# The causal mask of a score bank: written by ScalarE instead of by an identity product on TensorE

## What is computed

```python
x = x + _layernorm(attn(_layernorm(x)))
x = x + _layernorm(ffn(_layernorm(x)))          # ternary weights, hidden width 2048
# in attn, for each batch and head:
q, k = rope(q), rope(k)
scores = q @ k.T                                 # 512 x 512, where key > query: -inf
attn = softmax(scores) * E ** -0.5
o = attn @ v
```

## Time and profile before

| | |
|---|---|
| Median of 3 runs | 1364.31 us (1363.02 to 1364.67) |
| The profiled execution | 1362.21 us, its span 1360.4 us |
| Granted TensorE clock, mean over the span | 0.951 |
| PE busy | 1205.2 us (89%), 9388 instructions |
| DVE busy | 1025.1 us (75%), 2931 instructions |
| ACT busy | 782.3 us (58%), 1446 instructions |
| POOL busy | 593.8 us (44%), 636 instructions |
| PE on the chain that ended last | 56% of the span |

### The profile page before, as it was taken

One profiled execution on the slowest core, in us unless ns is written; L12 is line 12 of the kernel. 1 busy time (PEld: TensorE's weight loads), 2 busy tenths in 40 slices (PEclk: granted clock), 3 DMA queues, 4 the chain that ended last, 5 costly groups with the idle time before them and its releaser, 6 DMA issues.

```text
span 1360.4 us, 27331 instructions
## 1 busy us (share of the span) xinstructions
PE 1205.2 (89%) x9388; PEld 653.4 (48%) x9388; DVE 1025.1 (75%) x2931; ACT 782.3 (58%) x1446; POOL 593.8 (44%) x636
## 2 busy tenths in 40 slices
PE   4755869999999998999989998999989999988796
PEld 2322545455545554555545554555545554555343
DVE  7588897878887787878877787878877787767532
ACT  3334864666466754666456754666456754666480
POOL 5231432791159312881149412781149412871252
PEclk9865999999999999999989999999989999989799
DMA  5451121002210212002300212002300112001000
GB/s 201 127 153 64 41 62 55 1 4 68 81 38 2 56 53 82 1 18 66 105 3 2 55 46 89 1 14 66 94 18 2 49 48 61 1 2 46 17 2 31
DMA packets 49701, 65.60 MB, mean 48 GB/s; under 512 B 8439, under 2 KB 33047, under 8 KB 49052
## 3 DMA queue, kind: packets, MB, share of 16 engines
q1 hardware_dynamic: 49564, 63.78, 16.1%
HBM read 29.90 MB, written 8.39 MB: 28 GB/s over the span
## 4 chain that ended last, share of the span: by engine, by line
PE 56%; DVE 26%; ACT 7%; issue 6%; POOL 3%; DMA 1%; SPq 1%; POOLq 0%; ACTq 0%; DVEq 0%
PE gen L476 25%; PE down L519 14%; DVE score L1075 5%; PE pv L573 4%; PE score L545 4%; DVE hT L942 2%; PE score L536 2%; DVE acc_add L1052 2%; PE score L551 2%; DVE probs L942 2%; POOL rstd L1407 1%; DVE qkn L1167 1%; DVE mx L1075 1%; ACT qkn L736 1%; PE gen L536 1%
## 5 line engine op out<-in xcount | busy, mean ns | idle before, releaser
L1407 POOL TENSOR_TENSOR rstd<-veps,mhalf 128x1 f32<-128x1 f32 (+1 forms) x104 | 68.4, 657 | 492.9 <-DVE veps L1152 379.9
L792 ACT ACTIVATE probs<-score 128x512 f16<-128x512 f32 (+1 forms) x384 | 201.9, 526 | 127.5 <-PE score L545 127.5
L942 DVE TENSOR_TENSOR probs<-score,probs 128x512 f16<-128x512 f32 (+1 forms) x384 | 213.6, 596 | 65.6 <-ACT score L794 64.6
L476 PE MATMUL gen<-x2T,t1T 128*128 128x512 f16 x1024 | 249.9, 391 | 4.9 <-DVE hT L942 3.4
L519 PE MATMUL down<-t2T,hT 128*128 128x512 f16 x1024 | 232.8, 380 | 3.8 <-DVE xn L1137 3.8
L794 ACT ACTIVATE score<-score 128x512 f32<-128x512 f32 (+1 forms) x384 | 204.7, 533 | 0.0
L476 PE MATMUL gen<-xT,wa 128*128 128x512 f16 x768 | 178.2, 383 | 12.2 <-DVE wa L962 8.4
L942 DVE TENSOR_TENSOR hT<-gen,hT 128x512 f16<-128x512 f32 x160 | 109.0, 688 | 75.5 <-ACT gen L755 34.1
L1075 DVE CUSTOM_DVE_ANT_0 score<-score,mask_rows 128x512 f32<-128x512 f32 (+1 forms) x344 | 157.9, 522 | 0.0
L476 PEld LDWEIGHTS gen<-x2T,t1T 128*128 128x128 f16 x1024 | 99.1, 100 | 114.9 <-issue 14.0
L754 ACT ACTIVATE hT<-gen,gam 128x512 f16<-128x512 f32 x128 | 87.9, 687 | 115.1 <-PE gen L476 115.1
(11 more groups left out here) (131 smaller groups left out, 1863.0 us busy)
## 6 DMA issues: line engine op xcount, KB each, us to landing
qk<-qkn SPq DMA_DIRECT2D x384, 64.0 KB, 2.0
xo<-x SPq DMA_DIRECT2D x8, 1024.0 KB, 5.2
hT<-x SPq DMA_DIRECT2D x8, 1024.0 KB, 6.4
out<-xn SPq DMA_DIRECT2D x32, 256.0 KB, 2.1
hT<-w_fc SPq DMA_DIRECT2D x4, 1024.0 KB, 6.6
hT<-w_down SPq DMA_DIRECT2D x4, 1024.0 KB, 4.9
hT<-w_attn SPq DMA_DIRECT2D x4, 512.0 KB, 10.3
hT<-w_attn SPq DMA_DIRECT2D x1, 1024.0 KB, 8.9
```

The lines of the kernel that those rows point to most:

```text
L476: mm = nc.tensor.matmul(bank[:, :], a, b, start=(start and n == 0), stop=(stop and n == len(pairs) - 1))
L792: nc.scalar.activation(probs[:, h % 2, HI, 512 * i:512 * i + n], score[i][:, 0:n], ACT.Exp, scale=1.0 / S_UP)
L942: return V.tensor_tensor(out, whole, hi, ALU.subtract)
```

## The change

The identity product at the head of `scores` is gone. ScalarE writes the repeated mask into bank 0 with one copy (`mask_bank`), and announces it with a new semaphore `mask_set`, on which TensorE waits before the four diagonal score blocks; these are added onto what ScalarE wrote. The copy for head h+1 stands in `exponents(h)` between the exponentials of head h's second and third bank, and waits until VectorE has drained head h's first bank, which is what TensorE's `claim_score` waited for. The copy for head 0 stands right before `exponents(0)`, after the up stage.

```diff
@@ -270,7 +270,7 @@
         c_full, c_ready = sem("c_full"), sem("c_ready")
 
         g_full, g_drained = sem("g_full"), sem("g_drained")
-        s_full, s_drained = sem("s_full"), sem("s_drained")
+        s_full, s_drained, mask_set = sem("s_full"), sem("s_drained"), sem("mask_set")
         pv_full, pv_drained = sem("pv_full"), sem("pv_drained")
         down_full, down_drained = sem("down_full"), sem("down_drained")
         hsum_full, hsq_full = sem("hsum_full"), sem("hsq_full")
@@ -547,10 +547,8 @@
                     if h == 0:
                         pe.wait_ge(k_rows, 16)
                         pe.wait_ge(shift_rows, 32 * (j + 1))
-                    bank = claim_score(("scores", h), 0)
-                    nc.tensor.matmul(bank[:, :].rearrange("p (b t) -> p b t", b=TB), identb[:, :],
-                                     mask_b[:, :].unsqueeze(1).to_broadcast([PARTS, TB, PARTS]),
-                                     start=True, stop=False, skip_group_check=True)
+                    pe.wait_ge(mask_set, HEADS * j + h + 1)
+                    bank = score[0]
                     for s in range(TB):
                         mm = part(bank, PARTS * s, s, PARTS * s, PARTS * (s + 1), False)
                     mm.then_inc(s_full, 1)
@@ -785,9 +783,17 @@
                     high(qkn[:, g % 2, 1 + which, :], bank[:, :], bias=qk_bias[:, EC * which + g:EC * which + g + 1]
                          ).then_inc(qk_hi, 1)
 
+                def mask_bank(h):
+
+                    need(act, s_drained, s0 + S["scores", h] - 2)
+                    nc.scalar.activation(blocks(score[0]), mask_b[:, :].unsqueeze(1).to_broadcast([PARTS, TB, PARTS]),
+                                         ACT.Copy).then_inc(mask_set, 1)
+
                 def exponents(h):
 
                     for i, n in enumerate(SCORE_W):
+                        if i == 2 and h + 1 < HEADS:
+                            mask_bank(h + 1)
                         act.wait_ge(s_full, s0 + S["scores", h] + i + 1)
                         nc.scalar.activation(probs[:, h % 2, HI, 512 * i:512 * i + n], score[i][:, 0:n], ACT.Exp,
                                              scale=1.0 / S_UP)
@@ -870,6 +876,7 @@
                         if X_AT[u] + 2 < TB:
                             normalise(X_AT[u] + 2)
                 if here:
+                    mask_bank(0)
                     exponents(0)
                 if nxt and not here:
                     for c in range(EC):
```

## The result

The changed kernel takes 1412.59 us (1410.38 to 1413.41, 4 runs) where the kernel before takes 1364.49 (1363.02 to 1364.81). The ratio is 1.035, 95% interval 1.033 to 1.037: **48 us slower**, where 35 slower was forecast. The profiled execution has a span of 1410.2 us, 49.8 more than before.

A forecast was written before the change was run, and what follows sets the result against it. TensorE bound the middle head stages, almost without a wait, other engines close behind (slack 0.27 us). Losses 7 + 6 x 4.25 + 2.7 = +35 us on 1362.2 gave 1397, as median 1399 us; range 1368 to 1418.

The forecast's parts named there:

- Sign and mechanism: 2.6% slower: third-bank exponentials queue on ScalarE behind copy and its wait, delaying third subtraction, previous head's output and weighing.
- that slack: Middle stage, head 3: outputs allow weighing only 0.27 us before TensorE arrives, against a third subtraction 0.47 later.
- on-time and late rules: Third subtraction's end per head: 0.47 us later if VectorE is free early, 0.75 later if exponentials wait for VectorE.
- E + 3.60: On-time head: third subtraction ends 3.60 us after the head's first exponential starts (E), before at E + 3.13.
- D + 2.36: Late head: third subtraction ends 2.36 us after VectorE becomes free (D), before at D + 1.61.
- Weighing of head 3 at 18.96: Middle stage: head 3's weighing ready 18.96 us after head 0's scores start; TensorE there at 18.24.
- The scores of heads 1 to 11 of a middle stage: Start of each head's scores, new less old, from head 0's scores: -0.22 us at head 1 to +1.92 at head 11.
- The copy's price: ScalarE's turn for one 512-wide mask copy, taken as 0.50 us; floor 0.27, ceiling 0.60.
- Rival C: Middle stages: waits cut TensorE's busy share, the clock falls, 3.3 us lost per stage, 1419 us; chance 0.09.
- its term of +2.7: Batch 7: ScalarE and VectorE bind eight heads without down products, +4.3 us, less 0.22 in seven covered heads.
- Its first copy was costed at 1.1: Batch 0, head 0: ScalarE comes late, so copy, score product and first exponential follow one another: +1.1 us.
- 25.5 + 2.7 + 7: Microseconds lost in six middle stages (4.25 each), batch 7 and batch 0, together +35.

The follow-up runs named there:

- e1: Changed kernel with the copy for head h+1 moved behind head h's third bank's exponentials: 1364.67 us, 1.001 of the kernel before.
- e2: Kernel before, identity product kept, plus ScalarE's mask copy into an unread spare tile with the change's wait for VectorE: 1411.51 us, ratio 1.035.
- e7: Changed kernel with GpSimd's squares of hidden units 1 to 15 and final sums cut to one column: 1392.37 us, ratio 1.022.
- e4: Changed kernel with the mask copy on VectorE, behind its first bank's subtraction, instead of on ScalarE: 1393.54 us, 1.022 of the kernel before.
- e8: Changed kernel with eight unread 512-wide products in front of the next scores in batch 7's heads 1-4, 7, 8, 11, 12, 15: 1406.72 us, ratio 1.032.
- e9: Changed kernel with the last score product of batch 0's heads 1 to 15 issued nine times instead of once: 1415.07 us.
- e10: e5 with five unread 512-wide products before the scores in batch 7's heads without down products: 1350.30 us, 0.990 of the kernel before.
- e3: e2 without the wait for VectorE's subtraction; the spare copy waits only for the previous copy: 1376.14 us, 1.009 of the kernel before.
- e5: Changed kernel, copy behind the third bank, only nine heads per middle batch and six of batch 7; identity product elsewhere: 1352.98 us, 0.9925 of before.

## Why the prediction was right, and where it was short

**Sign and mechanism: right, and shown.** The measured 1412.59 lies in the range of 1368 to 1418, but just beyond what the forecast gave its own errors (1383 to 1412), and the loss is 48 where 35 was forecast. The step on which all hung was that slack: 0.27 us at the weighing of head 3, against 0.47 to 0.75 of delay on a path that the identity product's 0.22 does not shorten. e1 and e2 show it from both sides for the middle stages, which are 29 of the 48.6 us.

**The on-time and late rules: right in size.** On time, forecast E + 3.60; measured in head 2, where the first exponential starts at 776.51 and the third subtraction ends at 780.13, 3.62:

```profile
776.51 0.59 ACT L798 ACTIVATE probs<-score 128x512 f16<-128x512 f32 x1
779.71 0.42 DVE L949 TENSOR_TENSOR probs<-score,probs 128x256 f16<-128x256 f32 x1 [0.40 <-ACT score L800]
```

Late, forecast D + 2.36; measured 782.25 to 784.59, 2.34. Weighing of head 3 at 18.96 after the stage's start; measured 785.14 - 766.15 = 18.99. The scores of heads 1 to 11 of a middle stage: forecast -0.22, -0.44, -0.68, -0.17, +0.33, +0.20, +0.20, +0.46, +0.95, +1.71, +1.92; measured -0.21, -0.42, -0.65, -0.14, +0.36, +0.14, +0.12, +0.53, +1.03, +1.74, +1.93.

**The copy's price: right.** Taken 0.50. In the relay the third pair starts 0.54 after the copy (782.96, 783.50). The Trainium skill's formula (ScalarE: Activation LUTs, What ACT_TABLE_LOAD costs) gave 0.52, nearer than mine by the row. The 0.04 that mine is short is 0.3 us over some eight late heads of a stage.

**Middle stages: short by 0.7, from a term that was left constant.** I let VectorE's scaling into xo keep its length of 0.29 in the maxima heads. With GpSimd's two steps cut down, all 128 keep it (e7). The delays moved it beside GpSimd's final sum, and the sum moved as well, as ScalarE's normalisation is queued behind the held pair; I had followed that queue for head 7 alone. The term was worth 0.95 in head 11; e7 shows 1.1 per stage. That the stage is off by only 0.7 means that the other terms were some 0.3 too large from head 12 on. The Trainium skill (SBUF — State Buffer, Who interferes with whom) says that a VectorE instruction with two SBUF inputs contends with GpSimd's reads. By that rule, xo should have been checked against GpSimd's rows at each new place. The trace agrees: 1.26 beside GpSimd's sum, 0.29 without it; the subtractions, with one input in PSUM, keep their length.

**Rival C: the right mechanism, mostly in other stages.** I asked whether the clock would fall in the middle stages and held that short waits speak against it. In the profiled execution it was so: their granted clock stayed at 1.00 with TensorE busy 74.5 of 82 us. It isn't always so: in e4, e7, e8 and e9 one or two middle stages lost 0.7 to 1.3 us to a fall at head 7, far less than the 3.3 per stage of rival C. Also, batch 7 had shown 0.90 already; that it would fall further where TensorE does only scores and weighings between longer waits was not in its term of +2.7. It was worth about 4.4 of the loss, and 5.6 could be had back (e8). The Trainium skill (TensorE: Matmul & The Clock Gate, Part 1) says that activity releases the throttle; e8 and e10 agree, 0.79 to 1.00 and 0.92 to 1.00 by products that nobody reads. In e9 the added products left it at 0.78.

**Batch 0: short by about 4, cause partly open.** Its first copy was costed at 1.1; by the rows the cast of x ends its turn at 134.60, the copy, the score products (135.34) and the first exponential (135.96) follow, so the exponential comes 1.36 after the end of that turn; before, it came at once (133.67). The stage's clock is 0.77 after and 0.90 before, and in head 7 the twelve q/k products take 4.32 where they took 2.75. That the clock is the rest is argued, not shown, as e9 failed to raise it. The cast itself starts 0.94 later than before, which isn't explained; in e2 and e3, whose instructions up to there are those of the kernel before, the stage starts 1.4 and 1.2 later.

**The sum.** Forecast 25.5 + 2.7 + 7 = 35; measured 29.1 + 8.6 + 10.9 = 48.6. The 13 us too few are 3.6 in the middle (GpSimd and xo), 5.9 in batch 7 (about 4.4 the clock, the rest mostly xo beside GpSimd's squares, where e7's heads 3 and 4 turn in 3.30 instead of 3.76) and 3.9 in batch 0.

## What to carry to other kernels

An instruction moved to an idle engine brings its waits into that engine's queue: ask what stands behind it, and put it behind the work that others wait for, not in front. Read the slack of each wait in the profile before removing work in front of it: what was removed here was worth 0.22 at nine places of sixteen in a middle stage, and all sixteen together gave no more (e1: 1.7, e5: 1.9). When a change makes TensorE wait in a stage that already shows a granted clock under 1, cost the stage at the lower clock too.

## What the runs showed of the hardware that I had not expected

- In heads 3 and 4 of batch 7 VectorE's head loop ran in step with GpSimd's squares: the relay repeated every 3.76 us, as GpSimd's three instructions per hidden unit did, because each scaling into xo was held until the end of one of them (0.99 instead of 0.29). With GpSimd's squares cut down (e7) it repeated every 3.30 us.
- Products that nobody reads made a stage shorter by 5.6 us (e8) and by 1.4 us (e10); the granted clock of the stage rose to 1.00 with them, the level of 2.4 GHz.
- A fall of the clock in a busy stage can be there in one batch and not in the next of the same execution: in e7 the q/k products of head 7 took 4.08 us in one middle stage and 2.75 in the five others.
- In this kernel score products issued without a start flag add to what ScalarE wrote into the bank (-1e30 and zeros). Each column of the bank had been written by products of the up stage before; a bank where that isn't so was not run.
